# A ternary layer in another order with one rounding step on GpSimd, and top-64 attention whose old probabilities follow the next scores

## What is computed

```python
def bitlinear(x, W, b):
    w_scale = jnp.clip(jnp.mean(jnp.abs(W)), EPS, None)
    Wq = _ste(W, jnp.clip(jnp.round(W / w_scale), -1.0, 1.0) * w_scale)
    x_scale = jnp.clip(jnp.max(jnp.abs(x), axis=-1, keepdims=True), EPS, None)
    xq = _ste(x, jnp.clip(jnp.round(x * (QB / x_scale)), -QB - 1.0, QB) * (x_scale / QB))
    return jnp.einsum('bnd,hd->bnh', xq, Wq) + b
h = bitlinear(x, W1, b1)          # 256 -> 1024
h = jax.nn.gelu(h, approximate=False)
return bitlinear(h, W2, b2)       # 1024 -> 256
...
scores = jnp.einsum('bhqd,bhkd->bhqk', qh, kh) / np.sqrt(DHEAD)   # 16 heads, 77 keys
vals, idx = jax.lax.top_k(scores, 64)
probs = jax.nn.softmax(scores where kept, axis=-1)
ctx = jnp.einsum('bhqk,bhkd->bhqd', probs, vh)
return ctx @ wo_w.T + wo_b
```

## Time and profile before

| what | value |
|---|---|
| median of the 3 timed executions | 901.47 us (896.49, 901.47, 901.56) |
| profiled execution: its own time, its span | 897.16 us, 895.4 us |
| outside the span | 1.8 us |
| busy share of the span: PE, DVE, ACT, POOL | 89%, 73%, 56%, 59% |
| mean granted TensorE clock | 0.968 |
| ternary layer, steps 12 to 18 on DVE | about 221.6 to 273.7 us |
| top-64 attention, items 0 to 31 on DVE | 273.7 to 488.4 us |

### The profile page before, as it was taken

How to read it: one execution, slowest core, us unless ns; L and a number is a source line. 1 busy time by engine, 2 the same in 40 slices (tenths; PEclk the granted TensorE clock), 3 DMA queues, 4 the chain that set the end, 5 groups by cost and what they waited for, 6 DMA issues and landing times.

```text
span 895.4 us, 18961 instructions
## 1 busy us (share of the span) xinstructions
PE 801.0 (89%) x5858; PEld 628.7 (70%) x5858; DVE 655.2 (73%) x2739; ACT 497.2 (56%) x1287; POOL 531.4 (59%) x721
## 2 busy tenths in 40 slices
PE   6999998998788676867887989999999999998897
PEld 5677775886566444645666779788778879987775
DVE  4888686888979999999999873455455542516887
ACT  5778764568997797978877331222112122226673
POOL 3565644676752978878775125456455545237883
PEclk9999999999999697979999899999999999999999
DMA  9200001000000082000222621222222243140011
GB/s 296 62 1 2 2 1 48 1 1 1 1 1 1 2 328 97 1 25 2 71 72 87 227 72 36 37 42 43 37 42 43 36 87 58 19 107 1 13 36 48
DMA packets 37823, 46.70 MB, mean 52 GB/s; under 512 B 4327, under 2 KB 33871, under 8 KB 37724
## 3 DMA queue, kind: packets, MB, share of 16 engines
q1 hardware_dynamic: 29243, 35.77, 11.9%
q0 software_dynamic: 8480, 9.72, 7.1%
HBM read 33.80 MB, written 11.68 MB: 51 GB/s over the span
## 4 chain that ended last, share of the span: by engine, by line
PE 64%; DVE 14%; ACT 8%; issue 6%; POOL 6%; another core or an unknown queue 1%; DMA 1%; DVEq 0%; ACTq 0%; POOLq 0%; SPq 0%
PE ps L3012 10%; PE ps L3023 10%; PE ps L2358 4%; PE ps L2454 3%; PE ps L2481 3%; PE ps L2780 3%; PE ps L2800 3%; PE ps L3067 2%; PE ps L3041 2%; PE ps L2439 2%; ACT ptall L1254 2%; PE ps L2466 2%; DVE experts L1812 1%; PE ps L2811 1%; PE ps L2866 1%
## 5 line engine op out<-in xcount | busy, mean ns | idle before, releaser
L2080 DVE COPY ptall<-experts 128x512 f32 x136 | 53.3, 434 | 97.8 <-PE ps L3012 49.1
L1388 ACT ACTIVATE wk<-ps 128x1024 f32<-128x1024 f32 x34 | 34.9, 1025 | 131.3 <-PE ps L3012 69.1
L3012 PE MATMUL ps<-xnT,ptall 128*128 128x128 f32 x896 | 105.0, 275 | 2.3 <-DVE ptall L2080 1.8
L3012 PEld LDWEIGHTS ps<-xnT,ptall 128*128 128x128 f32 x896 | 102.4, 192 | 3.0 <-issue 3.0
L3023 PE MATMUL ps<-experts,wk 128*128 x448 | 102.0, 381 | 1.4 <-ACT xkeep L1398 1.4
L3023 PEld LDWEIGHTS ps<-experts,wk 128*128 128x128 f32 x448 | 82.9, 190 | 17.0 <-issue 6.8
L848 POOL DMA_INDIRECT xn<-expert_in,rown x34 | 36.0, 1058 | 80.7 <-PE ps L2998 57.1
L646 POOL TENSOR_TENSOR experts<-experts,rden 128x616 f32<-128x616 f32 x32 | 38.9, 1217 | 46.8 <-DVE rden L1572 46.8
L872 POOL DMA_INDIRECT token_sum<-xkeep,dest x28 | 47.6, 1699 | 31.1 <-ACT xkeep L1398 22.5
L1229 ACT ACTIVATE experts<-experts 128x77 f32<-128x77 f32 x248 | 62.1, 258 | 0.0
L2358 PE MATMUL ps<-ones 128*128 128x256 bf16 x434 | 55.7, 286 | 5.8 <-POOL mone L599 5.8
(11 more groups left out here) (382 smaller groups left out, 2358.5 us busy)
## 6 DMA issues: line engine op xcount, KB each, us to landing
experts<-in_ew SPq DMA_DIRECT2D x16, 1024.0 KB, 8.5
xkeep<-in_bw SPq DMA_DIRECT2D x2, 1024.0 KB, 7.3
expert_in<-xkeep SPq DMA_DIRECT2D x8, 256.0 KB, 3.9
x<-token_sum SPq DMA_DIRECT2D x8, 256.0 KB, 3.8
out<-x SPq DMA_DIRECT2D x7, 256.0 KB, 2.2
x<-in_x SPq DMA_DIRECT2D x1, 1536.0 KB, 9.1
token_sum<-x SPq DMA_DIRECT2D x4, 256.0 KB, 2.6
token_sum<-x SPq DMA_DIRECT2D x1, 1024.0 KB, 4.5
```

Of the source, the lines that this page charges most:

```text
L2080: ins = nc.vector.tensor_copy(tilew[:, v, c, :], experts[:, bass.ds(e * EW + (c * FF + v * 512), 512)])
L3012: ins = nc.tensor.matmul(ps[j % 2][:, v, k * P:(k + 1) * P], tilew[:, v, c, k * P:(k + 1) * P], xTb[j % 3][:, c, :], start=c == 0, stop=c ...
```

## The change

1. `mid_magic(b, 1)` goes from ACT to POOL: a tensor_scalar (multiply, add) on the same 128x1024 tile behind the scales in `mid_hidden`. `mid_magic(b, 0)` stays on ACT.
2. The order in a ternary step: on DVE `mid_scaled(k - 10, 0)` now stands ahead of `mid_largest(k - 11, 1)`, on PE `mid_first(k - 10, 0)` ahead of `mid_second(k - 13, 1)`.
3. Top-64 attention up to step LAST = 30: PE runs `top_values(k - 3)` right behind `top_scores(k + 2)`, then the output product, then the turning and the queries of the next pair, and `top_probs(k - 2)` last. ACT copies the probabilities of item k - 3 right behind the scores, ahead of the exp, and `top_out` goes behind the exp.
4. The next pair's queries keep their steps on PE from step 8 on, and come one step later for the second pair; ACT takes them in the step in which PE makes them.
5. `warm(14, 4)` is left out at steps 26 to 29. The turned tokens of the first early logits get a place of their own in the `experts` tensor.

```diff
@@ gpsimd, mid_hidden
                 nc.gpsimd.tensor_tensor(fac, fac, mone[:, 0:1], ALU.pow).then_inc(ghs, 1)
+                if t:
+                    gp.wait_ge(ghs, TB * b + t + 1)
+                    gp.wait_ge(ghq, TB * b + t)
+                    if b:
+                        gp.wait_ge(ght, TB * b + t - 1)
+                    nc.gpsimd.tensor_scalar(hmag[t], hbuf[b % 2][t], fac, MAGIC, ALU.mult, ALU.add
+                                            ).then_inc(ghq, 1)
@@ scalar, ternary steps
-                    if 0 <= k - 11 < B:
-                        if k == B + 10:
-                            top_queries(0, 1)
-                        mid_magic(k - 11, 1)
+                    if k == B + 10:
+                        top_queries(0, 1)
@@ scalar, top-64 steps
-                    q, j = (k - 1) // ITEMS + 1, (k - 1) % ITEMS
-                    if k >= 3 and (k - 3) // 2 % 2:
+                    ahead = k >= TURN_EARLY
+                    q, j = (k - 1 + ahead) // ITEMS + 1, (k - 1 + ahead) % ITEMS
+                    if k > LAST and (k - 3) // 2 % 2:
                         top_out(k - 3)
...
                     if 1 <= k < N4 - 1:
                         top_scores(k + 1)
+                    if 3 <= k <= LAST:
+                        top_turned_probs(k - 3)
                     if 1 <= k < N4:
                         top_exp(k - 1, 0)
...
+                    if 3 <= k <= LAST and (k - 3) // 2 % 2:
+                        top_out(k - 3)
                     if k in top_parts:
                         top_residual(top_parts[k] // 4, top_parts[k] % 4, k)
-                    if 2 <= k < N4 + 2:
+                    if LAST <= k < N4 + 2:
                         top_turned_probs(k - 2)
@@ vector, ternary steps
+                    if 0 <= k - 10 < B:
+                        mid_scaled(k - 10, 0)
                     if 0 <= k - 11 < B:
                         mid_largest(k - 11, 1)
...
-                    if 0 <= k - 10 < B:
-                        mid_scaled(k - 10, 0)
@@ tensor, top_probs
-                    if N4 - 9 <= i < N4 - 1:
+                    if N4 - 9 <= i < N4 - 1 and i + 2 not in top_parts:
                         warm(14, 4)
@@ tensor, ternary steps
+                    if 0 <= k - 10 < B:
+                        mid_first(k - 10, 0)
                     if 0 <= k - 13 < B:
                         mid_second(k - 13, 1)
-                    if 0 <= k - 10 < B:
-                        mid_first(k - 10, 0)
@@ tensor, top-64 steps
+                    if 3 <= k <= LAST:
+                        top_values(k - 3)
                     if k in top_parts:
                         top_final(top_parts[k] // 4, top_parts[k] % 4, k)
+                    if q + 1 < PAIRS:
+                        step = j + (k >= TURN_EARLY)
+                        if step == 4:
+                            top_turn(q + 1)
+                        if step in (5, 6):
+                            top_queries(q + 1, step - 5)
                     if 2 <= k < N4 + 2:
                         top_probs(k - 2)
...
-                        top_values(k - 2)
+                        if k >= LAST:
+                            top_values(k - 2)
...
-                    if q + 1 < PAIRS:
-                        if j == 3:
-                            top_turn(q + 1)
-                        if j in (4, 5):
-                            top_queries(q + 1, j - 4)
```

More of the change, by code:

```diff
@@ L225, in build @@
         mrow = arena(NK // 2).bitcast(bf16)
+        xt_first = arena(CH * S)
         mcol = sb("mcol", [P, B])
@@ L444, in build @@
                      for q in range(PAIRS - 1) for m in range(4)}
+        LAST = N4 - 2
+        TURN_EARLY = ITEMS
         l5_at = {16: 0, 20: 1, 24: 2, 28: 3}
         l5_logit_at = {23: 0, 27: 1, 31: 2}
-        xT5 = [wk[0][:, CH * h:CH * h + CH, :].rearrange("p c s -> p (c s)").rearrange("p (t c s) -> p t c s", t=TB, c=CH)
-               for h in (1, 0, 0, 0)]
+        xt_rest = wk[0][:, 0:CH, :].rearrange("p c s -> p (c s)")
+        xT5 = [v.rearrange("p (t c s) -> p t c s", t=TB, c=CH) for v in (xt_first, xt_rest, xt_rest, xt_rest)]
         def l5_cols(b):
@@ L1190, in top_queries @@
                         ac.wait_ge(done[3].sem, done[3].past(TT))
-                    elif q == 3 and p == 0:
-                        ac.wait_ge(lg_p.sem, lg_p.past(1))
                     for m in range(CH):
@@ L2787, in top_probs @@
                 def top_probs(i):
-                    q, j = (i + 1) // ITEMS + 1, (i + 1) % ITEMS
+                    q, j = (i + 2) // ITEMS + 1, (i + 2) % ITEMS + (i + 2 >= TURN_EARLY)
                     pe.wait_ge(pt_s[4].sem, pt_s[4].past(i))
-                    if N4 - 9 <= i < N4 - 1:
+                    if N4 - 9 <= i < N4 - 1 and i + 2 not in top_parts:
                         warm(14, 4)
                     pe.wait_ge(nm_s, i + 1)
-                    if q < PAIRS and j == 3:
+                    if q < PAIRS and j == 4:
                         pe.wait_ge(xts[4].sem, xts[4].past(2 * q + 2))
-                    elif q < PAIRS and j in (4, 5):
-                        pe.wait_ge(q_s[4].sem, q_s[4].past(4 * q + 2 * (j - 3)))
+                    elif q < PAIRS and j in (5, 6):
+                        pe.wait_ge(q_s[4].sem, q_s[4].past(4 * q + 2 * (j - 4)))
                     for h in range(HG):
@@ L2806, in top_values @@
                     s2 = j // 2 % 2
+                    if i - 1 in l5_at:
+                        pe.wait_ge(xts[5].sem, xts[5].past(l5_at[i - 1] + 1))
                     pe.wait_ge(pt_s[4].sem, pt_s[4].past(i + 1))
@@ L2940, in _ @@
                             l5_flip_half(l5_at[k - 2], k)
-                        if k - 3 in l5_at:
-                            pe.wait_ge(xts[5].sem, xts[5].past(l5_at[k - 3] + 1))
                         if k == N4:
```

## The result

The changed kernel takes 903.81 us (median of 12, 901.30 to 907.52), the kernel before 901.32 us beside it (median of 12, 896.49 to 904.15). The ratio is 1.0042, 95% interval 1.0022 to 1.0062, so 2 to 5.6 us slower. The forecast was 900 us and a change of 0.0 us by its sum; the measured time lies inside its range of 893.5 to 908, but the change is clear of noise. The profiled execution took 902.56 us, its span 900.8 (895.4 before). The profiled execution before, at 897.16 us, is 4.2 us under its median and this one 1.3 us under its own, so the 5.4 us between the two traces overstate the change.

The account below looks back on a forecast made before the run. VectorE was taken to bound the attention, ScalarE and VectorE in turn the ternary layer. Ternary +2.8 and attention -2.8 sum to 0.0 us on the profiled 897.16; forecast 900 us, between that and the median, range 893.5 to 908.

Parts of the forecast that it names:

- The bounds: VectorE limits the top-64 attention; the ternary layer is limited by ScalarE, then VectorE, then ScalarE, with sums deciding steps 13-17.
- Part 1: Ternary layer: rounding on GpSimd relieves ScalarE, ending VectorE's waits for exp and gelu at step 11; -1.2 us (0 to -1.5).
- Part 2: Ternary layer, steps 13 to 17: the new order leaves VectorE idle between the two sums; +4.0 us (2 to 5.5).
- the hole: Ternary layer, steps 13 to 17: VectorE idle 1.2 to 1.3 us between the two sums, ahead of the second.
- Part 3: Top-64 attention: the new order removes most ScalarE waits, cutting VectorE's 3.8 us of waits to 1.0; -2.8 us (-3.8 to +4).
- the 22.3 us of waits: Top-64 attention: ScalarE's waits for TensorE's turned probabilities, forecast to go nearly entirely, to under 5 us.
- The second rival: Top-64 attention wins nothing: ScalarE's waits move to queries and output product, VectorE keeps 3.8 us; +2.8, 903 us; chance 0.17.
- The third rival: Top-64 attention, steps 11-13 and 19-21 and the second pair's: half-clock TensorE costs about 6 us; 908 us and up; chance 0.15.
- The wait of 1.61 us ahead of item 31: Top-64 attention: the largest single wait ahead of an item on VectorE, 1.61 us, expected to go.

Follow-up runs that it names:

- run 1: Kernel before with only the ternary layer's second half-block rounding moved from ScalarE to GpSimd; 897.01 us, ratio 0.9973 to the kernel before.
- run 5: Changed kernel with TensorE's turning and queries put ahead of the old-probabilities product and last product; 898.86 us, ratio 0.9992 to the kernel before.
- run 7: Changed kernel with TensorE's queries ahead of the old product and ScalarE's old-probabilities copy ahead of the scores copy; 897.64 us, ratio 0.9978 to the kernel before.
- 4: Changed kernel with ScalarE's copies of the turned block and queries moved behind the second half of the exponentials; 905.01 us, ratio 1.0048 to the kernel before.
- 6: Changed kernel with only ScalarE's copy of the old probabilities moved ahead of its copy of the scores; 897.53 us, ratio 0.9981 to the kernel before.
- run 3: Changed kernel with its ternary layer put back as before, leaving only the top-64 change; 901.03 us, ratio 1.0016 to the kernel before.
- run 8: Changed kernel with VectorE's largest magnitude placed between the two sums of a ternary step; 898.36 us, ratio 0.9984 to the kernel before.
- run 10: Changed kernel with the old ternary order, GpSimd's rounding kept, and both top-64 moves (queries first, old-probabilities copy first); 893.54 us, ratio 0.9921 to the kernel before.
- 9: Kernel before with only the changed top-64 part, including both moves (queries first, old-probabilities copy first); 895.53 us, ratio 0.9962 to the kernel before.

## Why the prediction was wrong

- **The bounds** were read rightly: VectorE in the attention, and steps 13 to 17 of the ternary layer in the chain of the two sums. VectorE's busy time in the attention is unchanged, and what was won or lost was its idle time.
- **Part 1** (-1.2 us) held: -1.2 us in the layer by run 1, in the changed kernel itself 0.8, and TensorE was at half clock at step 12 there and the sum waited 0.36 us (in run 5, with the same layer at full clock throughout, it is 1.1). The size of the operation was off, 1.12 us for 2.0, and so was its lower bound of 1.2: an operation with two inputs at 616 elements doesn't bound one with a single input at 1024. Neither changed anything, as the working said. By the Trainium skill, GPSIMD Engine Reference, section 4.1, a one-input operation is near line rate there; the trace agrees, with 1.12 us for 1024 columns beside 1.22 for 616 with two inputs.
- **Part 2** (+4.0 us) held in the hole and in every step: +3.9 over steps 13 to 17. The layer came out at +3.1 for +2.8, in an execution with some half clock in it.
- **Part 3** (-2.8 us) is the step that failed: +2.5 us to item 31. Its first half was right: the 22.3 us of waits went. What failed is "VectorE only feels it when ScalarE is more than 3.5 us late. I come to some 2 us late at step 13, and over the edge by under 1 us around step 21 ... I leave 1.0 us of waits". It was 6.1 us, and 2.1 of them already stood at items 14 and 15. The 3.5 us as such are right: in run 7 the scores lie ready up to 3.5 us ahead of their item. Wrong was ScalarE's lateness: 2.2 us at step 11, ahead of the queries, and 4.4 at step 13, where I had 2. I had laid the pieces of one step in a row and asked how late its end is. The pieces lead back to the start of the same piece in the next step, at 7.3 to 7.45 us a turn against 6.37, and so the lateness adds up over the steps with turning and queries. At step 11, at half clock, the turning of probabilities took 1.96 us and ScalarE waited 0.81 for it, so the first turn didn't start on time either. Runs 4 to 7 show the ring: the same ring in another place costs the same (4), 0.64 us less in it makes the kernel 4.5 us faster (5), 0.7 us less or both 5.5 and 5.8, with no wait left (6, 7). By the times too it is this part that is off: run 3 gives +0.16% (-0.10 to +0.42), 1.4 us slower, for a forecast of 2.8 us faster.
- The second rival, in which the waits move to the queries, was the right mechanism. Its 903 us for 903.8 are luck in part: it starts from 900 us, 1.3 under the median beside the changed kernel, and it kept VectorE's waits at 3.8, where they grew. The reason that I gave for it, ScalarE's wait for GpSimd, was not the cause: in run 7 ScalarE waits 23.9 us for GpSimd's shifted scores ahead of the magnitude, for 7.0 before, and VectorE doesn't wait.
- The third rival, the half clock, is not the whole cause, and not excluded as a part. The mean clock of the attention, 0.91, is no lower than before, and a ring that is shorter by 0.7 us took all waits away. But a stretch at 0.50 lies at steps 11 and 12, the place that the rival named, and the wait ahead of item 14 goes with its length in the three traces with this ring and this place of the queries: 0.93 us with 6.8 us of it (changed kernel), 2.49 with 10.2 (run 3), 3.07 with 10.3 (run 8). At the next pair another stretch, 416.4 to 419.9 us, lies ahead of items 22 to 24, which waited 3.05 us; in run 3, at 1.00 from 409.1 to 470.5 us, only item 23 waits, 1.66 us. That much the ring costs at full clock, and how the rest is shared between ring and clock stays open. What the prediction read ahead of the clock's fall, a wait of 2.22 us at 301.36, lies inside the slow stretch and not ahead of it.
- The rest of the difference between the traces, 1.3 us ahead of the ternary layer and -1.5 us behind item 31, is within the spread that the same code shows in the thirteen traces. The wait of 1.61 us ahead of item 31 went as forecast, and so did nearly all of the 22.3 us.

## What to carry to other kernels

When an engine's wait is taken away by handing it an older result, ask what the freed order puts behind that engine's step. If a chain of pieces on two engines leads within one step from a copy back to the same copy of the next, add it up all round and hold the sum against the limiting engine's time for a step: over it, lateness grows with every turn. Then ask how late the feeding engine is when the first turn begins, not only how late it may be. Here taking a piece out of the ring helped, and moving a wait along it did not. Between two users of one bank, 1.2 us of other work hid a product of 1.03 us; which of two works stands there can be chosen so that the other one comes earlier, as in run 8.

## What the hardware showed that I had not expected

TensorE's clock falls to its lower level in some executions and not in others at the same place of the same code. Runs 1 and 10 have the same ternary layer, which starts 1.1 us later in run 10. These are the windows of the same ten microseconds of it in run 1 and in run 10:

```profile
232.00:242.00 10.00, 7.19 (x54) 5.20 (x51) 9.97 (x21) 7.11 (x10) 8.35 (x18) 1.00 0.01 2
```

```profile
233.10:243.10 10.00, 7.86 (x48) 5.63 (x47) 9.05 (x20) 6.79 (x9) 7.86 (x18) 0.83 0.01 2
```

In the first TensorE has 1.00 and VectorE is busy 9.97 us, in the second 0.83 and 9.05: it waits 0.71 us ahead of a sum at 238.08, which it did not in run 1. The whole layer took 64.48 us in the one and 65.63 in the other. And the ternary layer of the kernel before, unchanged in runs 3 and 9, took 65.66, 65.90 and 67.68 us, at a granted clock of 0.974, 0.974 and 0.950. So a layer's length in one trace is good to about 2 us here, and effects of that size need the medians of several executions, or a stretch short enough to see what the clock did in it.
